# A graph layer and a routed FFN on one core: the order of the norm statistics, node sums and distance operands, first differences on VectorE, the raw taps in other buffers, two ranks behind the FFN's first operand

## The reference, cut to what matters

```
x [8, 1024, 128]; adj [8, 1024, 1024] of zeros and ones

x = x + gnn(layernorm(x), adj)
x = x + ffn(layernorm(x))

gnn: h = relu(bn1(conv1(xT)));  h = bn2(conv2(h, 17 taps));  x_conv = relu(h + xT)
     s = x w_se + b_se (3 wide); A = exp(-|s_n - s_m|^2) * adj
     x_nmp = A relu(x w_msg + b_msg)
     GRU of [x_conv, x_nmp] with the state x
ffn: weights = x wr + br; of each batch the 511 rows with the largest weights
     are updated: gelu(row w1 + b1) w2 + b2, times the row's weight
```

## Time and profile before

| what | us |
|---|---|
| median of three runs | 657.58 (656.57 to 659.09) |
| the profiled execution, its own time | 657.72 |
| its span, first to last instruction | 655.7 |
| around the span | 2.0 |
| PE, DVE, ACT, POOL busy | 558.6, 489.9, 352.7, 301.0 |
| mean granted clock of PE | 0.954 |

### The profile page before, as it was taken

How to read it: one execution, slowest core, us unless ns; L and a number is a source line. 1 busy time by engine, 2 the same in 40 slices (tenths; PEclk the granted TensorE clock), 3 DMA queues, 4 the chain that set the end, 5 groups by cost and what they waited for, 6 DMA issues and landing times. The chain is left out here.

```text
span 655.7 us, 8975 instructions
## 1 busy us (share of the span) xinstructions
PE 558.6 (85%) x2928; PEld 421.2 (64%) x2928; DVE 489.9 (75%) x1044; ACT 352.7 (54%) x607; POOL 301.0 (46%) x376
## 2 busy tenths in 40 slices
PE   2959998899888988898889978996999878699980
PEld 1856797568745885588557955795569755566640
DVE  7866477588978896889698869886978876958620
ACT  3916583656455655756374737582757352445540
POOL 4522252325338343835363635564436235056773
PEclk9979998899989998999899999999899988989995
DMA  7160600071006300450036001700070004403120
GB/s 249 44 245 1 256 1 1 0 270 53 1 0 215 139 1 1 142 213 1 0 90 264 1 1 46 277 1 0 28 274 21 1 1 128 146 21 109 49 84 28
DMA packets 34397, 55.84 MB, mean 85 GB/s; under 512 B 2338, under 2 KB 23861, under 8 KB 34224
## 3 DMA queue, kind: packets, MB, share of 16 engines
q1 hardware_dynamic: 30256, 48.95, 21.6%
q0 software_dynamic: 4096, 6.33, 2.8%
HBM read 44.74 MB, written 14.75 MB: 91 GB/s over the span
## 5 line engine op out<-in xcount | busy, mean ns | idle before, releaser
L760 ACT ACTIVATE tr<-D 128x512 f32<-128x512 f32 x128 | 76.4, 597 | 149.1 <-PE D L1424 114.0
L1430 PEld LDWEIGHTS M<-cst,adjb 128*128 128x128 f32 x512 | 65.5, 147 | 80.1 <-DVE ga L1079 36.8
L1430 PE MATMUL M<-cst,adjb 128*128 128x128 f32 x512 | 82.5, 286 | 35.9 <-DVE ga L1079 26.9
L1424 PE MATMUL D<-V,U 128*128 128x512 f32 x128 | 95.4, 746 | 13.4 <-DVE V L1047 7.0
L1079 DVE TENSOR_TENSOR ga<-tr,M 128x512 f32<-128x512 f32 x64 | 43.7, 682 | 51.9 <-POOL wk L606 30.5
L556 POOL DMA_INDIRECT sel<-R,ridx x64 | 64.7, 1010 | 20.2 <-issue 17.0
L1453 PE MATMUL N<-ga,msgF 128*128 128x512 f32 x128 | 72.1, 658 | 0.0
L1453 PE MATMUL N<-tz,msgF 128*128 128x512 f32 x128 | 64.2, 593 | 0.0
L1308 PE MATMUL C<-zR,wc 128*128 128x256 f32 x208 | 61.3, 295 | 1.6 <-DVE zR L993 1.6
L1309 PE MATMUL C<-zR,wc 128*128 128x256 f32 x208 | 59.4, 285 | 0.0
L1310 PE MATMUL C<-zR,wc 128*128 128x256 f32 x208 | 59.2, 284 | 0.0
(11 more groups left out here) (230 smaller groups left out, 1552.9 us busy)
## 6 DMA issues: line engine op xcount, KB each, us to landing
adjb<-in_adj SPq DMA_DIRECT2D x7, 4096.0 KB, 14.3
adjb<-sel SPq DMA_DIRECT2D x8, 516.0 KB, 4.9
out<-R SPq DMA_DIRECT2D x8, 512.0 KB, 3.5
xall<-in_x SPq DMA_DIRECT2D x7, 512.0 KB, 5.4
adjb<-in_adj SPq DMA_DIRECT2D x1, 2560.0 KB, 10.1
adjb<-in_conv_w SPq DMA_DIRECT2D x1, 1088.0 KB, 7.4
adjb<-in_adj SPq DMA_DIRECT2D x1, 1024.0 KB, 9.9
sel<-R,ridx POOLq DMA_INDIRECT x64, 2.4
```

Of the source, the lines that this page charges most:

```text
L760: nc.scalar.activation(E[:, u % NE, :], Db[u % NH][:, :], ACT.Exp, scale=-1.0).then_inc(exp_ok, 1)
L1424: MM(Db[h][:, :], U[:, t * P:(t + 1) * P], V[:, half(h)], start=True, stop=True).then_inc(d_ps, 1)
L1430: i = TR(Mb[h][:, k * P:(k + 1) * P], adjb[:, h * TH + k, t * P:(t + 1) * P], ident)
```

## The change

It has seven parts.

1. POOL: the `statistics2` of the state's norm move from between the two halves of `residual` to behind both; EF2's differences move ahead of `state_less_candidate`.
2. DVE forms EF1 itself (two instructions of 128x260 a batch, new semaphore `ef1_ok`), which POOL did. ACT takes EF1's and EF2's high parts one place earlier.
3. DVE: `common_added(b, 0)` moves behind all four distance operands and the state's sums; `distance_operands` 0 and 1 stand ahead of EF3's low part; `common_of_b` stands between the halves of `distance_lo`; `blend` stands behind EF2's low part.
4. Units: `normalise2` one unit earlier, `conv_hi` and the first `conv_lo` one earlier, rank tile 6 one later, `indices` at unit 13 in place of 10, `moments1` at 14.
5. Start: the raw taps go to R and W, which the ranks use later. The first adjacency is loaded in two parts: tiles 2 to 7 at once, 0 and 1 behind the gates' low parts. The low part of batch 0's features comes ahead of the parameters, and the pair sums of taps on POOL wait for it.
6. End: rank tiles 6 and 7 of batch 6 and its second `indices` move from the last `step` into the FFN's first step, behind the low part of the first gathered rows.
7. End, POOL: the first four scatters of batch 6 stand ahead of `state_less_candidate(7, 1)`.

```diff
-AHEAD_AT, BEHIND_AT = {3: 5, 6: 6, 9: 7}, {5: 5, 8: 6, 10: 7}
+AHEAD_AT, BEHIND_AT = {3: 5, 7: 6, 9: 7}, {5: 5, 8: 6, 10: 7}
-N2_AT = (6, 7, 8, 9)
+N2_AT = (5, 6, 7, 8)
...
+        raw_t = R[:, :, :, :].rearrange("p k t r -> p (k t r)")[:, 0:(N_TAP - 2 * KQ) * D]
+        raw_p = W
...
-            load_adj0(T0_TAPS, T0_FREE, W_TAPS + 1)
-            load_adj0(0, T0_TAPS, W_GATES + 1)
+            load_adj0(0, T0_FREE, W_GATES + 1)
...
             def step(b, q, first, last):
-                differences_of_b(b)
                 differences(b, 0)
+                differences_of_e(b)
                 if not first:
                     state_less_candidate(b - 1, 1, 1 - q)
-                differences_of_e(b)
                 differences(b, 1)
                 differences_of_f(b)
                 residual(b, q, 0)
-                if not first:
-                    statistics2(b - 1)
                 residual(b, q, 1)
                 if first:
                     statistics1(1)
                 else:
+                    statistics2(b - 1)
                     row_numbers(b - 1, 1 - q)
...
                 if first:
+                    rows_by_rank(B - 2, 0, 0)
                     state_less_candidate(B - 1, 1, 1)
-                    rows_by_rank(B - 2, 0, 0)
...
+            def differences_of_b(b):
+
+                wait(dve, ab_ok, b, NH, NH)
+                wait(dve, q1_ok, b - 1, NH, NH)
+                z = hab[:, 1, :]
+                TT(EF1[:, 0:LQ], phase(z, 0), phase(z, 1), ALU.subtract)
+                TT(EF1[:, LQ:2 * LQ], phase(z, 2), phase(z, 1), ALU.subtract).then_inc(ef1_ok, 1)
...
                 if not first:
                     new_gate(b - 1, 1)
+                differences_of_b(b)
                 lo_of_odd(b, 0, hab[:, 1, :], ZB)
                 lo_of_pair(b, 0, EF1, ZEF1)
...
-                else:
-                    blend(b - 1, 1)
                 lo_of_pair(b, 1, EF2, ZEF2)
                 if first:
                     lo_of_weights(W_GATES)
-                distance_lo(b, q)
+                else:
+                    blend(b - 1, 1)
+                distance_lo(b, q, 0)
                 common_of_b(b)
+                distance_lo(b, q, 1)
                 lo_of_odd(b, 0, fF, ZF)
-                common_added(b, 0)
+                distance_operands(b, q, (0, 1))
                 lo_of_pair(b, 0, EF3, ZEF3)
-                distance_operands(b, q, (0, 1, 2))
                 if not first:
                     state_to_nodes(b - 1, Mb)
-                distance_operands(b, q, (3,))
+                distance_operands(b, q, (2, 3))
+                common_added(b, 0)
...
-                        if u == 10:
-                            indices(b - 2, q, 1)
...
-                    if u == 13 and b + 2 < B:
+                    if u == 13 and b > 1:
+                        indices(b - 2, q, 1)
+                    if u == 14 and b + 2 < B:
                         moments1(b + 2)
...
                 if last:
-                    for t in range(5, T):
-                        rank(b - 1, 0, t)
-                    indices(b - 1, 0, 1)
+                    rank(b - 1, 0, 5)
...
                     lo_of_sel(0, 0)
+                    rank(B - 2, 0, 6)
+                    rank(B - 2, 0, 7)
+                    indices(B - 2, 0, 1)
                     blend(B - 1, 1)
```

More of the change, by code:

```diff
@@ L574, in phase_differences @@
                 nc.gpsimd.tensor_tensor(ef[:, LQ:2 * LQ], phase(z, 2), phase(z, 1), ALU.subtract).then_inc(z_ok, 1)
[L576 to L580, removed]
             def differences(b, k):
-                if k == 0 and b > 1:
-                    pool.wait_ge(rank_ok, T * (b - 2) + T - 3)
+                if k == 0:
+                    wait(pool, ab_ok, b, NH, NH)
+                    if b > 1:
+                        pool.wait_ge(rank_ok, T * (b - 2) + T - 3)
                 z = (eF, fF)[k]
@@ L589, in differences_of_e @@
             def differences_of_e(b):
-                wait(pool, z_ok, b, 5, E_AT)
+                wait(pool, z_ok, b, N_DIFF, E_AT)
                 wait(pool, xT_ps, b, NH, NH)
@@ L595, in differences_of_f @@
             def differences_of_f(b):
-                wait(pool, z_ok, b, 5, F_AT)
+                wait(pool, z_ok, b, N_DIFF, F_AT)
                 wait(pool, zL_ok, b, NZ, ZEF1)
@@ L670, in hi_of_pair @@
             def hi_of_pair(b, z, src, n):
-                wait(act, z_ok, b, 5, n)
+                if n == 0:
+                    wait(act, ef1_ok, b, 1, 1)
+                else:
+                    wait(act, z_ok, b, N_DIFF, n)
                 if n == EF3_AT:
@@ L823, in step @@
                 hi_of_odd(b, 0, hab[:, 1, :], ab_ok, NH, NH)
-                if not first:
-                    candidate(b - 1, 1)
                 if first:
@@ L828, in step @@
                     hi_of_weights(W_PAIRS)
-                hi_of_pair(b, 0, EF1, EF1_AT)
+                hi_of_pair(b, 0, EF1, 0)
+                if not first:
+                    candidate(b - 1, 1)
                 embed(b, q, 0)
-                hi_of_odd(b, 1, eF, z_ok, E_AT, 5)
-                embed(b, q, 1)
-                common_part(b)
+                hi_of_odd(b, 1, eF, z_ok, E_AT, N_DIFF)
                 hi_of_pair(b, 1, EF2, EF2_AT)
@@ L1031, in add_msg_bias, with distance_lo @@
                        bmsg.unsqueeze(1).broadcast_to([P, TH, D]), ALU.add).then_inc(mb_ok, 1)
-            def distance_lo(b, q):
+            def distance_lo(b, q, h):
                 sH, sL = xTH[:, 1 - q, :], xTL[:, 1 - q, :]
-                for h in range(NH):
-                    hs = half(h)
-                    wait(dve, sH_ok, b, NH, h + 1)
-                    TT(sL[:, hs], wk[:, hs], f32(sH[:, hs]), ALU.subtract).then_inc(sL_ok, 1)
+                hs = half(h)
+                wait(dve, sH_ok, b, NH, h + 1)
+                TT(sL[:, hs], wk[:, hs], f32(sH[:, hs]), ALU.subtract).then_inc(sL_ok, 1)
             def distance_operands(b, q, ns):
@@ L1180, in step @@
                         conv_sum(b, 1)
[L1181 removed]
+                    if u == 6:
                         conv_lo(b, 0)
```

47 lines of the change are left out of this document (29 added, 18 removed).

## The result

The changed kernel takes **583.23 us** (median of four runs, 582.88 to 583.74), beside 658.28 for the kernel before on the same chip: a ratio of 0.886, with a 95% interval of 0.884 to 0.889. The forecast was 592.4, its range began at 584. The change is faster, as forecast, and by 9 us more. In a later set it gave 583.49.

A forecast was written before the change was run, and what follows sets the result against it. PE was nearest to full, its waits paid some seven times. Seven batches gave 57.4 us, the start 3.0 and the end 4.9, together 65.3: 657.7 became 592.4 us, range 584 to 600 (chance 0.60).

The forecast's parts named there:

- EF1 cost 0.2 us: Each batch: forming EF1 on DVE lies in an idle stretch and costs 0.2 us, bounds 0 and 1.5.
- the ranks' 3.6 us: End: the FFN's first `up` no longer waits behind ranks 6 and 7 and the indices, 3.6 us gained.
- the transfers' 9.9 us as queueing: Start: a part's 9.9 us in its row was read as queueing; 1024 KB alone would take about 5.9.
- the forecast's 38.9: Start: the first front begins at 38.9 us against 41.98, from release at 33.0 plus 5.9 of transfer.
- DVE becomes the bound: Rival, in the batches: DVE's work and remaining waits set the pace, total 600 to 615 us; chance 0.20.
- The port: Rival: EF1 on DVE waits for POOL's instructions, all behind conv1 some 1.5 us late, total 601.5 us; chance 0.08.
- Per batch 6.07 + 2.3 - 0.2 = 8.2 us.: Batches 1 to 7: adjacency gains 6.07, first front 2.3, EF1 costs 0.2; 68.48 us becomes 60.3.
- since the weights stay at their unit: Adjacency, batches 1 to 7: PE still waits 0.97 us for the weights' row.
- Batch 0's 22.94 us: Unit 3 to first gate: batch 0's time as pace for later batches, plus 2.03 for the weights' row, so 24.97.
- The last batch ... I credit no more: The last batch, with more waits and its own rank ahead of unit 0, is credited only the usual 8.2 us.
- Start, 3.0: Start: the first front comes 3.0 us earlier; bounds a loss of 1 and a gain of 5.
- End, clock 1.3: FFN's first `up`: the clock may hold behind the shorter wait, gaining between nothing and 2.6 us; the middle, 1.3, taken.

The follow-up runs named there:

- number 1: The changed kernel with the state's norm between the two node sums again: 620.45 us.
- 3: The changed kernel with VectorE's old order: first node term ahead of the distance operands, three operands behind EF3's low part. 600.35 us.
- 5: The changed kernel with EF1's two instructions back on POOL, ahead of eF: 584.57 us.
- 7: The changed kernel with ranks 6 and 7 ahead of the FFN again: 587.31 us; its first run, on a chip with stops, 616.06.
- 6: The changed kernel with the raw taps back in the adjacency's buffer: 590.69 us; with 28 unread matmuls in TensorE's wait as well: 589.00 us.
- 8: The changed kernel with the parameters ahead of the low part of batch 0's features again: 580.92 us.
- 2: The kernel before with only the state's norm moved behind both node sums: 630.1 us.
- 9: The changed kernel with the weights' row one unit earlier: 579.07 us; with the odd low part ahead of EF1 as well: 586.28 us.
- 4: The kernel before with only the norm behind both node sums and the first node term behind the distance operands: ratios 0.915 and 0.917 on two chips.

## Why the prediction was right in kind and 9 us too high

**The chain of cause was right.** The node sum held unit 3, the norm held the node sum (number 1), and V and xall held the first front (3). EF1 cost 0.2 us and lay in an idle stretch (5). The first `up` came earlier by the ranks' 3.6 us (3.4 in 7). In the start, reading the transfers' 9.9 us as queueing was right: the last 1024 KB are issued at 33.57, land in 4.9 us, and the front starts at 38.56. That it is so near the forecast's 38.9 is partly luck: the issue came 0.6 us later than put down and the transfer was 1.0 us shorter.

```profile
adjb<-in_adj SPq DMA_DIRECT2D x1, 1024.0 KB, 4.9
```

**"DVE becomes the bound"** (0.20) fell: it is busy 55.9 of 59.66 us in a batch and TensorE waits 0.64. I had put its work at 54.9, and the rival kept 7.0 us of its waits; of the 11.35 us that it idled, 3.8 are left. **"The port"** (0.08): the second EF1 instruction was held up, at a price of 0.2 us and not 1.5.

**The steps that failed** are sizes of four terms, and they sum to the 9.2 us:

- *"Per batch 6.07 + 2.3 - 0.2 = 8.2 us."* It was 8.8, and 9.8 in batch 1. The 0.97 us for the weights' row, "since the weights stay at their unit", became 0.44: VectorE stands at that unit earlier. Batch 0's 22.94 us as the pace of the rest was exact. In batch 1 the kernel before also lost the clock behind V and xall (8.28 us from the first front to unit 3, at 0.79, where the other batches take 6.81): I let one batch stand for all. Together 4.7.
- *"The last batch ... I credit no more"*: 9.8 for 8.2, so 1.5. TensorE waited 8.7 us there in the kernel before (70.35 less 61.70), 3.71 of them at unit 3's stall and 1.84 for the weights' row, where the batch of the earlier trace rows has 3.06 and 0.97; 2.1 us are left.
- *Start, 3.0*: the first front gained 3.4, and the clock behind its wait another 2.0, which I left out although I counted the same thing at the end. The row was there: 7.33 us for what takes 5.33 at full clock. 2.4 too little. Two larger effects of opposite sign hid in the start: the placement gave 7.2 (6), the parameters' new place cost 2.6 (8).
- *End, clock 1.3*: the FFN gained 1.9, all in its first step (7). The slow clock had cost more than its twelve matmuls showed, 2.7 us with the two behind them; 1.3 of that goes into the wait for gn in the changed kernel, and a wait of 0.39 us for xall is gone with it. "Between nothing and 2.6 I take the middle" priced a chance and not a mechanism: the clock stayed at 1.00 in one trace of the changed kernel and fell in the other. That the number was near is luck.

And one thing that the total did not show: taken alone, the norm's move gains 28 us, where I would have said 43 (2). My sum priced each wait by itself, and gave back to the norm's move the clock that fell behind its stall. With the stall gone the clock fell at the next pair of waits instead; with both gone it stayed at 1.00 in all six batches of the changed kernel.

## What to carry to other kernels

Where an engine has two granted clocks, price a wait by its length and by the slower matmuls behind it, at every place where it stands (the start too), and don't add the gains of two moves when each leaves a wait that the clock falls behind. Before you credit the clock to a change, look at a second trace of the same kernel. When a small instruction is moved "out of the way", look at what it now runs beside: a gap that it filled costs nothing, and a neighbour on the shared port can make 0.16 us into 1.27. When the bound engine is near 99% busy, its last waits of 0.4 us a stage are still worth something: 4.4 of 583 us here (9).

## What the runs showed of the hardware that I had not expected

**The clock does not follow from the length of the wait alone.** After waits of 1.01 and 1.29 us TensorE ran at 1.00 in a batch of the kernel before, and at 0.50 for some 3.5 us in the same place of number 2; after 0.29 and 1.29 us it fell in batch 1 of number 3, and after 0.33 and 1.29 us it did not in batch 4. After the same 2.15 us ahead of `up` it stayed at 1.00 in one trace of the changed kernel and fell in the other (7). After 3.05 us and more it fell in each batch of the kernel before, but after 3.27 us in batch 1 of number 1 it stayed at 1.00. What decides it between such cases stays open.

**The same kernel took 657.5, 670.3 and 683.4 us on three chips.** The expectations say that all engines stood still; the trace of number 7's first run shows it more exactly. VectorE stops for 3.53 us, and ACT close behind it for 3.77, with nothing to wait for that the profile knows:

```profile
247.40 0.69 DVE L1093 TENSOR_TENSOR ga<-tr,M 128x512 f32<-128x512 f32 x1 [3.53 <-issue]
```

POOL's gathers go on meanwhile, and TensorE, with work in stock, waits 1 us. It begins in batch 2, and the FFN has stops of up to 10 us. The cause stays open. For the comparison it means that a difference of 4 us can't be read there, and a ratio only within 1% (4); undisturbed stretches can be compared.
